# A graph network on one core: 56 instead of 48 edge tiles are summed ahead of the feature table, four between two ordinary tiles in place of two, and a table's block is stored by one transfer

## The reference, cut to what matters

```python
# N = 3125 nodes, D = 128 features, 53125 edges sorted by destination, 8 edge types
h = relu(layernorm(x))
for W, root, bias in three_layers:  # relational graph convolution
    out = h @ root + bias
    for r in range(8):
        msg = where(edge_type == r, (h @ W[r])[src], 0)
        agg = segment_sum(msg, dst)
        cnt = segment_sum(edge_type == r, dst)
        out = out + agg / maximum(cnt, 1)
    h = relu(out)
x = x + h
h = relu(layernorm(x))                          # a second kind of layer
z = relu((h + segment_sum(h[src], dst)) @ W1 + b1) @ W2 + b2
return x + batchnorm(z) * gamma + beta + h
```

## Time and profile before

| | us |
|---|---|
| median of three runs | 1913.76 (1910.78 to 1917.29) |
| the profiled execution | 1917.36 |
| its span, first to last instruction | 1915.3 |
| TensorE busy | 1209.7 (63%) |
| GpSimd busy | 1201.2 (63%) |
| VectorE busy | 843.3 (44%) |
| ScalarE busy | 636.2 (33%) |
| mean granted clock of TensorE | 0.633 of full speed |

### The profile page before, as it was taken

The page is one execution under the profiler, slowest core; times in us unless marked ns, Lnnn a source line. Parts: engine busy times, 40 slices in busy tenths (PEclk is TensorE's granted clock), DMA queues, the critical chain, the costliest instruction groups (busy, mean ns, idle before and its releaser), DMA issues.

```text
span 1915.3 us, 17586 instructions
## 1 busy us (share of the span) xinstructions
PE 1209.7 (63%) x4604; PEld 856.7 (45%) x4627; DVE 843.3 (44%) x3270; ACT 636.2 (33%) x1147; POOL 1201.2 (63%) x1350
## 2 busy tenths in 40 slices
PE   6798764655565565656565656567566565656667
PEld 2266443434344354444444444446344444444444
DVE  4566575355444245655556566552121212122123
ACT  5310500000000256766767676752011020202133
POOL 5755666666666656666666666656666666666660
PEclk9697855555555655656565556565567676756688
DMA  7552333233322311222222222231111111111111
GB/s 226 180 159 89 85 113 93 78 106 89 93 87 73 101 38 43 84 51 79 57 72 61 72 64 67 66 93 47 44 47 44 50 43 48 46 45 44 47 47 40
DMA packets 80802, 144.19 MB, mean 75 GB/s; under 512 B 24687, under 2 KB 38248, under 8 KB 80696
## 3 DMA queue, kind: packets, MB, share of 16 engines
q0 software_dynamic: 39840, 81.67, 17.3%
q1 hardware_dynamic: 40424, 60.68, 9.2%
q10 hardware_dynamic: 432, 0.64, 0.1%
HBM read 100.23 MB, written 42.67 MB: 75 GB/s over the span
## 4 chain that ended last, share of the span: by engine, by line
another core or an unknown queue 29%; PE 25%; issue 15%; POOL 14%; DVE 7%; ACT 6%; DMA 2%; DVEq 0%; SPq 0%; ACTq 0%; POOLq 0%
POOL rows L1250 14%; PE ps_agg L561 7%; PE ps_h L530 6%; PE ps_a L648 4%; DVE early L1059 3%; ACT scratch L845 3%; DMA rows<-h_table,idx 2%; DVE sel L963 2%; PE ps_agg L616 1%; PE ps_a L579 1%; DVE scratch L1048 1%; PE ps_a L668 1%; PE ps_h L668 1%; ACT early L1337 1%
## 5 line engine op out<-in xcount | busy, mean ns | idle before, releaser
L1250 POOL DMA_INDIRECT rows<-h_table,idx x1175 | 1118.7, 952 | 631.2 <-issue 323.8
L561 PE MATMUL ps_agg<-sel,rows 128*128 128x64 f32 (+14 forms) x2764 | 664.8, 362 | 280.2 <-DMA rows<-h_table,idx 210.3
L561 PEld LDWEIGHTS ps_agg<-sel,rows 128*128 128x128 f32 x2764 | 625.2, 287 | 459.3 <-DMA rows<-h_table,idx 245.6
L963 DVE TENSOR_SCALAR sel<-iota,early,norm 128x64 f32<-128x64 f32 x1178 | 357.0, 334 | 427.1 <-PE ps_agg L561 208.8
L648 PE MATMUL ps_a<-scratch 128*128 128x300 bf16 x416 | 165.5, 399 | 255.7 <-DVE early L1059 142.5
L1059 DVE TENSOR_TENSOR early<-ps_a,early 128x300 f32 x416 | 195.9, 471 | 261.7 <-remote 177.2
L845 ACT ACTIVATE scratch<-scratch,ones 128x300 bf16<-128x300 f32 x416 | 221.2, 532 | 161.7 <-remote 129.2
L530 PE MATMUL ps_h<-w_all,xT 128*128 128x512 f32 x300 | 220.7, 849 | 59.7 <-issue 24.1
L851 ACT ACTIVATE scratch<-iota,code_lo 128x300 f32<-128x300 f32 x416 | 226.5, 545 | 12.5
L941 DVE TENSOR_SCALAR_CACHE_REDUCE agg_s<-scratch,key_f 128x256 bf16<-128x256 int16 x416 | 193.5, 472 | 31.5 <-issue 20.5
L648 PEld LDWEIGHTS ps_a<-scratch 128*128 128x128 bf16 x416 | 59.7, 144 | 296.9 <-issue 283.6
(11 more groups left out here) (158 smaller groups left out, 739.7 us busy)
## 6 DMA issues: line engine op xcount, KB each, us to landing
h_table<-stage SPq DMA_DIRECT2D x130, 256.0 KB
rows<-h_table,idx POOLq DMA_INDIRECT x1175
scratch<-key_rows SPq DMA_DIRECT2D x26, 544.0 KB
h_table<-scratch SPq DMA_DIRECT2D x20, 256.0 KB
x_rows<-in_x SPq DMA_DIRECT2D x6, 256.0 KB, 6.1
w_all<-in_W SPq DMA_DIRECT2D x3, 512.0 KB, 6.7
x_table<-early SPq DMA_DIRECT2D x6, 256.0 KB, 2.3
out<-early SPq DMA_DIRECT2D x6, 256.0 KB
```

Of the source, the lines that this page charges most:

```text
L561: mm = nc.tensor.matmul(sums_of(L, k)[:, at:at + width], mine, sel[edges, G % SELS, in_window:in_window + width], start=False, stop=(t == ...
L963: done = nc.vector.tensor_scalar(mine, here, dst, weight, ALU.is_equal, ALU.mult)
L1250: pool.indirect_dma_start(rows[:, slot, :], None, table, bass.IndirectOffsetOnAxis(ap=column, axis=0)).then_inc(landed, 16)
```

## The change

FORE goes from 48 to 56 and FORE_PACE from 2 to 4. HEAD goes from 66 to 67, and the banks from 6 to 7. A block of a table is stored by one transfer of 512 KB, issued when both halves are copied, so every wait for stores counts 16 a block in place of 32.

```diff
-FORE = 48
+FORE = 56
 FORE_RING = 12
-FORE_PACE = 2
+FORE_PACE = 4
...
             if stores_of(slot_of[H], H):
-                eng.wait_ge(s_stage[slot_of[H]], 32 * stores_of(slot_of[H], H))
+                eng.wait_ge(s_stage[slot_of[H]], 16 * stores_of(slot_of[H], H))
...
             sp.wait_ge(s_evA, H + 1)
-            sp.dma_start(rows_out[:, 0:4, :], rows_in[:, 0:4, :]).then_inc(s_stage[slot_of[H]], 16)
             sp.wait_ge(s_evD, H + 1)
-            sp.dma_start(rows_out[:, 4:8, :], rows_in[:, 4:8, :]).then_inc(s_stage[slot_of[H]], 16)
+            sp.dma_start(rows_out, rows_in).then_inc(s_stage[slot_of[H]], 16)
...
```

More of the change, by code:

```diff
@@ L813, in fill @@
                 for n in range(STAGES):
-                    act.wait_ge(s_stage[n], 32 * stores_of(n, BLOCKS * GIN))
+                    act.wait_ge(s_stage[n], 16 * stores_of(n, BLOCKS * GIN))
             if b >= FILLS:
@@ L927, in late_tile @@
                 for n in range(STAGES, ALL_STAGES):
-                    dve.wait_ge(s_stage[n], 32 * stores_of(n, BLOCKS))
+                    dve.wait_ge(s_stage[n], 16 * stores_of(n, BLOCKS))
             if t >= 2:
@@ L1113, in wait_table @@
             for n in range(ALL_STAGES):
-                pool.wait_ge(s_stage[n], 32 * stores_of(n, BLOCKS * (L + 1)))
+                pool.wait_ge(s_stage[n], 16 * stores_of(n, BLOCKS * (L + 1)))
         SP_BRANCH = 7
@@ L1258, in _ @@
                         for n in range(ALL_STAGES):
-                            pool.wait_ge(s_stage[n], 32 * stores_of(n, table_of(L, late_blocks[0])))
+                            pool.wait_ge(s_stage[n], 16 * stores_of(n, table_of(L, late_blocks[0])))
                         pool.wait_ge(s_late_made, 1)
```

## The result

The changed kernel takes 1932.6 us in the median of 9 runs (1924.73 to 1938.32), the kernel before 1917.06 in 9 runs on the same chip: ratio 1.0077, 95% interval 1.0055 to 1.0099. It is slower by more than the 0.3% that can be told from no change. (The 1913.76 us in the sections ahead are the first three of the nine runs before.) The profiled execution took 1938.32 us (span 1936.4, granted clock 0.639), 5.7 above its median; the profiled one of before stood at 1917.36 (1915.3, 0.633).

The account below looks back on a forecast made before the run. TensorE's list of fore tiles and banks was taken to bound the head, POOL's gathers the rest of layer 0. 5.7 + 5.6 + 0.2 + 2.5 + 0.2 - 1.4 + 2.3 = 15.1 us on 1913.8 gave 1928.9, range 1918 to 1940.

Parts of the forecast that it names:

- (1): Start of the head: TensorE's first ordinary tile 5.7 us later, as DVE waits for chunk 4 of the keys.
- (2): Head: eight more fore tiles on TensorE at 0.70 us each, 5.6 us; the seventh bank's opening adds 0.2.
- (3): End of the head: a fourth key_banks of 64 columns, 2.5 us, plus 0.2 of waiting for its bank's copy.
- (4): Head: 12 ordinary tiles up to tile 67 in place of 20, 1.4 us less.
- (5): Head, behind the new idle time: TensorE's clock falls to its lower level, 2.3 us lost (0 to 5.3).
- The single store: Table stores: one transfer per block costs 0, with ends of -3 and +3 us for hand-overs before 105 us.
- (a): Rival: POOL is the bound throughout, the head too; eight gathers fewer save 10.0 us, 1904; chance 0.16.
- (b): Rival, layer 0 behind the head: up to 15 us of lateness vanish in its waits, 1914; chance 0.12.
- (c): Rival, head's start: keys come earlier, clock stays at 1.00; +7.8 us, 1921.6; chance 0.66 together with the forecast.
- (d): Rival, table 0: the later first half holds up staging buffers, 14.5 us on top, 1943; chance 0.05.
- (e): Rival: the edges' test, narrower with 56 tiles, sends the kernel into its slow general loop, many times the time; chance 0.01.
- The signs: Trace after: 6.5 us idle before TensorE's first ordinary tile, head's end at 177, gather 78 at 178.5, layer 0's end at 661.

Follow-up runs that it names:

- with the selections first: Changed kernel with VectorE's first eight selections made ahead of the matches that need the fifth chunk of keys: 1929.95 us, ratio 1.0083 (kind A); 1.012 on kind B.

## Why the prediction was right, point by point

The forecast was 1928.9 us, +15.1, for the reason that TensorE's work in the head is the bound there. The time was 1932.6, +15.5 against before's runs on the same chip; of the 3.7 us to the forecast, 3.3 are that before's median of nine runs lies above that of three. The mechanism held where it mattered: the head is longer, all behind it moves along, and the saved gathers save nothing. That the sum came within 1 us of the time is in part luck, since the head accounts for 12 to 13 us of it and several terms were off in opposite directions. By steps:

(1) The later start, 5.7 us. From L539 to the first ordinary tile it was 10.25 us (114.98 less 104.73) and is 14.03: +3.8. DVE did wait for the keys, but their chunk was there 9.5 us behind the head's opening (123.06 less 113.53), where 11.3 was forecast (116.0 less 104.73). In the second profile of the changed kernel it came 14.0 behind it (DVE's first match of chunk 4 stands at 109.86), and the later start is +8.5:
```profile
95.85 1.02 PE L539 MATMUL ps_agg<-xT,w_all 128*128 128x512 f32 x2
...
114.59 0.69 PE L561 MATMUL ps_agg<-sel,rows 128*128 128x64 f32 x2 [8.50 <-issue]
...
164.74 2.14 PE L590 MATMUL ps_agg<-hid,w_all 128*128 128x64 f32 x16 [0.73 <-ACT hid L741]
166.70 5.40 PE L561 MATMUL ps_agg<-sel,rows 128*128 128x37 f32 x26
```
(2) to (5) The rest of the head: forecast 5.6 + 0.2 + 2.7 - 1.4 + 2.3 = 9.4. From the first ordinary tile to the end it was 47.3 us and is 55.2, +7.9; in the second profile 52.1, +4.8. The whole head is 11.7 and 13.3 us longer, where 15.1 was forecast. The three stretches printed with the result divide this. Busy time times clock is the work at full clock: 41.4 us before, 48.5 and 49.2 after, so 7.0 and 7.8 more (to about half a microsecond, as the clock has two digits), where the terms (2), (3) and (4) without their waits make 6.9. The work was forecast well. What the clock took is 1.7 us before, 5.4 and 2.1 after: 3.7 and 0.3 more, forecast 2.3. What the prediction lacked is idle time: it read the head from a window at either end, 115 to 125 and 155 to 163, and took TensorE for busy all through. But between 134 and 145 it had waits of 3.4 us, and nothing like them stands there afterwards: 2.8 and 3.3 us less idle, where 0.2 more was forecast. What ended most of these waits the profile doesn't name, and why they went is open.

(3) The fourth bank, 2.5 us: its records took 3.65 us in the first profile and 2.14 in two others on kind A; in all seven profiles with this bank it is four times 2.14, and 3.28, 3.65 and 3.68. The clock makes the difference: 0.58, 0.55 and 0.50 in these three, each behind a wait of 0.73 us, as long as in the other four. At full clock 64 columns take 2.14 where 128 took 3.97, so the width does halve it; the weight loads don't set the pace.

(5) The clock: behind the gap 6.93 us busy at 0.50 lose 3.5 us, forecast 2.3; another 1.6 us are the fourth bank's (3.46 us busy at 0.55). That TensorE falls back behind such a gap is the rule of the Trainium skill, page TensorE: Matmul & The Clock Gate, section Why this matters for your kernels; the row of 125 to 135 agrees. Shorter waits were followed by a low clock here as well, in some executions: that of 1.61 us before 144.56 in the kernel before by 0.72 in 144 to 150, and those of 1.77 and 1.56 us with the selections first by 0.66 in 124.84 to 135.

The single store, 0: confirmed on kind B, twice. But the head of the profiled changed kernel opens 8.8 us late, and this the prediction had only as an end of ±3 us. The store with 56 tiles doesn't always bring it: the second profile of the same kernel, on another chip, opens at 95.85, 8.9 us earlier than the kernel before. On kind A the six openings lie between 95.70 and 113.60, on kind B all eight between 71.22 and 72.66. What decides it on kind A stays open, and with it whether what lies between the head's 12 to 13 us and the runs (+15.5 and +16.4 us by the medians, 15 and 20 by the ratios) is such chance, the store on kind A, or something behind the head. The profiles can't tell: one profile stands for each kernel and chip, and the stretch from the head's end to L616 alone differs by 4.8 us between two kernels on one chip (508.4 and 513.2). From L616 to the end it was 1238.7 us before and 1239.3 after on the first chip, and 1228.2 on the other.

The rivals. (a), POOL the bound throughout, is refuted by the times. Its premise is nearly right on kind B, where POOL sets the pace behind the head and its first gather the start, and it is still wrong there: it had counted the eight gathers saved behind table 0 and not the eight added ahead of it, which are POOL's too and as dear. (b) is refuted by the times, +15.5 and +16.4 us, and behind the head on kind B nothing near 15 us is made up (444.7 and 444.8 us with the old numbers, 443.5 and 443.9 with the new). On kind A the 514.3 us in both are one pair of profiles, and such a stretch can be 5 us off. The prediction's sum for it was loose: 405 us of gathers and 68.7 of waits are more than the 464 us of the stretch, since each of the 38 waits holds the 0.3 us of the step once more. (c), the wait off, was made by hand: the head gets 4 us shorter, and 1.0083 stands; whether the time gains them is open. (d) is refuted for kind B; on kind A no run has the store alone. (e) didn't come.

The signs. Forecast was a wait of about 6.5 us before the first ordinary tile, an end of the head at 177 and gather 78 at 178.5. The two profiles show 4.56 and 8.50, 182.77 and 166.70, 184.03 and 167.62. The second head ends below the 168 us that were to be the sign of an error, but only because it opened at 95.85. Points in time depend on the opening, which varies by 18 us on kind A; lengths would have been the better sign. From gather 78 to layer 1's first gather the profiles show 484.6 us before, 485.9 and 481.3 after, within the 5 us that were allowed.

## What to carry to other kernels

Taking gathers out of a stage in which their engine waits for another anyway can save nothing, and the gathers added elsewhere cost time if the engine is the bound there: count its waits in both places, and the added gathers as well as the removed. Read a stage whole before calling an engine its bound: two windows of it hid 4 us of idle time. And where one wait is taken away, look which comes next before counting the gain. Where an engine may be only a fixed number of tiles ahead of another, what counts at the end of a mixed stage is how many of the other's tiles are done and when. A lookahead by tile number that crosses a chunk's border adds the chunk's landing to the first tile, even where the tile itself doesn't need it.

## What was not expected of the hardware

One program took 1895 to 1917 us on some chips and 1650 on others; why, no run here shows. One place where it shows is the hand-overs of table 0: ScalarE's copies follow each other every 0.86 us on kind B, and on kind A every 1.4 to 3.6 us for a while, some with releasers that the profile can't name. Busy time of 50 to 60 us in the changed kernel (kind A), then in the kernel with the single store (kind B):
```profile
50.00:60.00 10.00, 6.81 (x7) 1.91 (x8) 4.16 (x19) 1.75 (x3) 7.87 (x20) 0.50 0.32 98
```
```profile
50.00:60.00 10.00, 9.51 (x25) 4.49 (x26) 9.94 (x39) 7.35 (x14) 9.03 (x21) 1.00 0.96 348
```
Both are in table 0: 7 instructions of TensorE in 10 us against 25, at a clock of 0.50 against 1.00. The bound differs too: on kind B POOL has 53% of the chain that ended last (single store alone), on kind A 14% in the kernel before and 22% in the changed one.
